# A post-norm decoder layer with routed experts: weights split by GpSimd beside the experts, a later order of units, and gate maxima spread by TensorE

## The reference

```
x = LN(x + Attn(x))                        # 16 batches x 128 tokens x 256, 16 heads of 64
x = LN(x + mLSTM(q=x, k=v=ctx))            # 4 heads of 64, gates from 3*256 features
   log_f = log_sigmoid(fg); cs = cumsum(log_f)
   log_d[t,s] = cs[t] - cs[s] + ig[s]  (s <= t);  m = max_s log_d;  d = exp(log_d - m)
   c = (q @ k.T / 8) * d;  h = c / (max(sum c, exp(-m)) + eps) @ v;  RMS norm per head
xn = LN(x) * gamma + beta;  probs = softmax(xn @ Wr + br);  top 2 of 8 experts
full[e] = relu(xn @ W1[e] + b1[e]) @ W2[e] + b2[e]      # W1 256x1024, W2 1024x256
c = relu(b1) @ W2 + b2;  out = sum_k score_k * (full[idx_k] - c[idx_k] + sum_e c_e)
x = LN(x + x + out)
```

## Time and profile before

| | us |
|---|---|
| runs | 919.39, 920.82, 922.27 (median 920.82) |
| profiled execution, its own time | 924.46 |
| its span, first to last instruction | 922.6 |
| PE / DVE / ACT / POOL busy | 710.0 / 441.9 / 331.3 / 307.8 |
| mean granted TensorE clock | 0.859 |

### The profile page before, as it was taken

The page is one execution under the profiler, slowest core; times in us unless marked ns, Lnnn a source line. Parts: engine busy times, 40 slices in busy tenths (PEclk is TensorE's granted clock), DMA queues, the critical chain, the costliest instruction groups (busy, mean ns, idle before and its releaser), DMA issues.

```text
span 922.6 us, 14727 instructions
## 1 busy us (share of the span) xinstructions
PE 710.0 (77%) x4774; PEld 600.5 (65%) x4775; DVE 441.9 (48%) x906; ACT 331.3 (36%) x994; POOL 307.8 (33%) x416
## 2 busy tenths in 40 slices
PE   5898898888787987986553102999999999699762
PEld 4788787778676785865443001788888888588421
DVE  3334444465363654647266600555555555255354
ACT  4565656656465565664121000222121212121100
POOL 3156335353645526356434174000000000000572
PEclk9899989989798999999555555999999999899755
DMA  9756454453434534354355432117427311510242
GB/s 308 281 184 191 130 160 149 138 162 108 131 104 153 165 98 129 94 164 138 105 226 205 195 107 80 35 58 286 183 83 295 149 40 40 227 35 24 69 142 75
DMA packets 87141, 130.22 MB, mean 141 GB/s; under 512 B 9856, under 2 KB 72752, under 8 KB 86064
## 3 DMA queue, kind: packets, MB, share of 16 engines
q1 hardware_dynamic: 81664, 83.36, 28.2%
q0 software_dynamic: 5408, 46.15, 13.1%
q10 hardware_dynamic: 16, 0.01, 0.0%
HBM read 79.12 MB, written 50.36 MB: 140 GB/s over the span
## 4 chain that ended last, share of the span: by engine, by line
PE 43%; POOL 14%; issue 14%; DMA 14%; DVE 9%; SPq 5%; ACT 1%; POOLq 0%; DVEq 0%; ACTq 0%
PE bank L881 11%; DMA w_dram<-w_pair 8%; PE bank L852 4%; PE bank L854 4%; PE bank L853 4%; PE bank L862 3%; POOL arena L654 3%; POOL w_pair L552 3%; PE bank L664 3%; PE bank L666 2%; PE bank L665 2%; POOL w_pair L550 2%; PE bank L805 2%; DMA y_dram<-work 2%; DMA w_raw<-in_L_ffn_b_dram 2%
## 5 line engine op out<-in xcount | busy, mean ns | idle before, releaser
L550 POOL CAST w_pair<-work 128x256 fp32r<-128x256 f32 x128 | 60.8, 475 | 184.1 <-DMA w_dram<-w_pair 164.5
L881 PE MATMUL bank<-w_ring,hidT_hi 128*128 x320 | 119.7, 408 | 1.3 <-DVE hidT_lo L1403 1.3
L1071 ACT ACTIVATE hidT_hi<-bank 128x512 fp32r<-128x512 f32 x80 | 43.6, 596 | 181.5 <-PE bank L862 181.5
L552 POOL TENSOR_TENSOR w_pair<-work,w_pair 128x256 fp32r<-128x256 f32 x128 | 103.0, 805 | 10.2
L994 ACT ACTIVATE arena<-bank,negmx 128x128 f32<-128x128 f32 x256 | 90.8, 375 | 20.8 <-DVE negmx L1108 20.8
L881 PE MATMUL bank<-w_ring,hidT_lo 128*128 x320 | 83.3, 281 | 0.0
L1376 DVE TENSOR_TENSOR arena<-bank,w_raw 128x512 f32<-128x512 f32 x80 | 55.3, 692 | 49.6 <-PE bank L854 48.8
L852 PE MATMUL bank<-w_ring,xgT_hi 128*128 x160 | 68.7, 430 | 11.3 <-DMA w_raw<-in_L_ffn_b_dram 8.5
L555 POOL DMA_DIRECT2D w_ring<-w_dram x8 | 4.7, 590 | 217.4 <-PE bank L881 217.4
L881 PEld LDWEIGHTS bank<-w_ring,hidT_hi 128*128 128x128 f32 x320 | 60.1, 188 | 12.9 <-issue 1.8
L1382 DVE TENSOR_REDUCE work<-bank 128x256 f32<-128x512 f32 x40 | 27.7, 692 | 80.9 <-PE bank L881 71.2
(11 more groups left out here) (215 smaller groups left out, 1854.2 us busy)
## 6 DMA issues: line engine op xcount, KB each, us to landing
w_dram<-w_pair SPq DMA_DIRECT2D x128, 256.0 KB, 2.3
w_ring<-w_dram POOLq DMA_DIRECT2D x8, 4096.0 KB, 12.9
work<-in_L_ffn_W_dram SPq DMA_DIRECT2D x128, 128.0 KB, 2.8
xg_dram<-work SPq DMA_DIRECT2D x10, 512.0 KB, 8.9
work<-xg_dram SPq DMA_DIRECT2D x40, 128.0 KB
y_dram<-work SPq DMA_DIRECT2D x40, 128.0 KB, 1.7
work<-gmax_dram SPq DMA_DIRECT2D x16, 256.0 KB, 3.9
w_raw<-in_L_ffn_b_dram POOLq DMA_DIRECT2D x8, 512.0 KB, 14.0
```

Of the source, the lines that this page charges most:

```text
L550: pool.tensor_copy(hi, raw).then_inc(w_rounded, 1)
L552: pool.tensor_tensor(lo, raw, hi.bitcast(F32), ALU.subtract).then_inc(w_split, 1)
L881: last = pe.matmul(o, l, r, start=c == 0 and l is both[0], stop=c == FC - 1 and l is both[0])
L1071: nc.scalar.activation(hidT_hi[:, par, 4 * half:4 * half + 4, :], bank[3 + half][:, :].rearrange("p (c t) -> p c t", c=4), ACT.Relu)\
```

## The change

The weights no longer pass through DRAM. `w_dram`, `gmax_dram`, the parts, `spread_maxima` and their buffers go. GpSimd loads an expert's raw weights into `w_raw` (two halves, W1 and W2, 1 MB each) and splits a half in one cast and one subtraction of 128x2048, straight into `w_ring`. The biases move to the place of `wq_lo`. The maxima are spread by a new unit B: four products of a 4x128 selector with gmax, into a ring bank which the decays then read. The lists of units, ScalarE's cut of them and VectorE's order change too.

```diff
             if s == 0:
-                return (of("S", i - 2) + of("k", i, 2) + of("q", i, 2) + of("w", i - 1, 1, 0),
-                        of("w", i - 1, 1, 1) + of("q", i, 3) + of("k", i, 3) + of("N", i - 4))
+                return (of("k", i, 2) + of("q", i, 2) + of("w", i - 1, 1, 0),
+                        of("w", i - 1, 1, 1) + of("q", i, 3) + of("S", i - 2) + of("k", i, 3) + of("N", i - 4))
             if s == 1:
-                return (of("v", i, 1, 0) + of("T", i - 2),
-                        of("v", i, 0, 1) + of("v", i, 1, 1) + of("L", i - 4) + of("X", i - 1) + of("C", i - 1))
+                return (of("v", i, 1, 0) + of("B", i - 2, 0),
+                        of("v", i, 0, 1) + of("B", i - 2, 1) + of("v", i, 1, 1) + of("L", i - 4) + of("T", i - 2))
             if s == 2:
-                return (of("x", i + 1, 0) + of("x", i + 1, 1) + of("G", i - 1) + of("q", i + 1, 0) + of("k", i + 1, 0),
-                        of("q", i + 1, 1) + of("k", i + 1, 1))
+                return (of("x", i + 1, 0) + of("x", i + 1, 1) + of("X", i - 1) + of("C", i - 1)
+                        + of("q", i + 1, 0) + of("k", i + 1, 0), of("q", i + 1, 1) + of("G", i - 1) + of("k", i + 1, 1))
...
# GpSimd
-            def load_expert(e):
-                pool.dma_start(w_ring[:, e % RING, :], w_dram[e]).then_inc(w_loaded, 16)
-                pool.dma_start(b1_rep[:, e % RING, :], b1[e:e + 1, :].broadcast_to([P, F])).then_inc(w_loaded, 16)
+            def load_raw(e, part):
...
+            def load_bias(e):
+                if e > 0:
+                    pool.wait_ge(b1_loaded, 16 * e)
+                pool.dma_start(b1_rep[:, e % RING, :], b1[e:e + 1, :].broadcast_to([P, F])).then_inc(b1_loaded, 16)
+
+            def split(e, part):
...
+                pool.wait_ge(w_loaded[part], 16 * e + 16)
+                pool.tensor_copy(both[:, :, 0, :], raw).then_inc(w_rounded, 1)
+                pool.wait_ge(w_rounded, 2 * e + part + 1)
+                pool.tensor_tensor(both[:, :, 1, :], raw, both[:, :, 0, :].bitcast(F32), ALU.subtract)\
+                    .then_inc(w_split, 1)
+                if e + 1 < E:
+                    pool.wait_ge(w_split, 2 * e + part + 1)
+                    load_raw(e + 1, part)
             def mask(p, b):
-                pool.wait_ge(decay_done, 2 * p + b + 1)
+                read(pool, ("B", p, b))
...
                     if s == 3 and 0 <= i - 3 < PAIRS:
                         scale_xn(i - 3)
+                    if (i, s) == (PAIRS - 1, 2):
+                        done(pool, ("v", PAIRS - 1, 1, 1))
+                        for part in range(2):
+                            load_raw(0, part)
+                    if (i, s) == (PAIRS - 1, 3):
+                        split(0, 0)
                     if (i, s) == (PAIRS, 1):
-                        load_expert(0)            # and experts 1 and 2 at (9, 1) and (10, 3)
+                        for k in range(RING):
+                            load_bias(k)
+                        split(0, 1)
+                    if (i, s) == (PAIRS, 2):
+                        split(1, 0)
                     if (i, s) == (PAIRS + 2, 3):
+                        split(1, 1)
+                        for part in range(2):
+                            split(2, part)
...
             for e in range(RING, E):              # each behind y_done of expert e - 3
-                load_expert(e)
+                load_bias(e)
+                for part in range(2):
+                    split(e, part)
# TensorE
+                elif kind == "B":
...
+                    for h in range(XH):
+                        last = pe.matmul(dst[:, h * S:(h + 1) * S], pick_head[:, h, :], gmax[:, b * S:(b + 1) * S],
+                                         start=True, stop=True)
             def hidden(j, par, half, e):
-                    pe.wait_ge(w_loaded, 32 * e + 32)
+                    pe.wait_ge(b1_loaded, 16 * e + 16)
+                    pe.wait_ge(w_split, 2 * e + 1)
             def expert_out(j, par, e, look):
+                pe.wait_ge(w_split, 2 * e + 2)
# ScalarE: decays(un) runs in the place of B's copy
-                    last = nc.scalar.activation(dec[:, b, h, :], dec[:, b, h, :], ACT.Exp,
+                    last = nc.scalar.activation(dec[:, b, h, :], ring(un)[0][:, h * S:(h + 1) * S], ACT.Exp,
...
-                    cut = {0: len(before) - 2, 1: 0, 2: 2, 3: 2}[s] if i < PAIRS else 0
+                    split = {0: 1, 1: 1, 2: 4, 3: 2}[s] if i < PAIRS else 0
+                    if s == 3 and 0 <= i - 1 < PAIRS:
+                        soft_gates(i - 1)         # was at the end of step 2
# VectorE, in step order
-                    if s == 1: weigh(i - 2)       # first in step 1
-                    if s == 2: read_gates(i - 1)  # ahead of add_heads
+                    if s == 3: both_norms(i - 3)  # now ahead of gate_sums(i - 1)
                     if n + 1 < STEPS * PAIRS:
                         weights_of(n + 1)
+                    if s == 1 and 0 <= i - 2 < PAIRS:
+                        weigh(i - 2)
+                    if s == 2 and 0 <= i - 1 < PAIRS:
+                        read_gates(i - 1)
```

More of the change, by code:

```diff
@@ L109, in decoder_layer @@
         w_raw = sb("w_raw", [P, W_WORDS])
+        wq_lo_at = nc.sbuf_base
         wq_lo = sb("wq_lo", [P, KC, INNER], F32R)
@@ L296, in decoder_layer @@
         gmax_ready = sem("gmax_ready")
-        gmax_stored = sem("gmax_stored")
+        pick_ready = sem("pick_ready")
         m_ready = sem("m_ready")
         em_ready = sem("em_ready")
-        mrep_loaded = [sem(f"mrep_loaded{k}") for k in range(2)]
-        decay_done = sem("decay_done")
         masked = sem("masked")
@@ L319, in decoder_layer @@
         scattered = sem("scattered")
-        part_loaded = [sem(f"part_loaded{k}") for k in range(4)]
-        pair_stored = [sem(f"pair_stored{k}") for k in range(2)]
-        w_loaded = sem("w_loaded")
+        w_loaded = [sem(f"w{k + 1}_loaded") for k in range(2)]
+        b1_loaded = sem("b1_loaded")
         w_rounded = sem("w_rounded")
@@ L432, in _ @@
                     .then_inc(zeros_stored, 16)
[L433 to L477, removed]
             for i in range(LAST):
@@ new lines, in load_bias @@
+            def load_bias(e):
[3 more added lines that the diff above has]
+            def split(e, part):
+                n = (512, D)[part]
+                half = slice(part * W_WORDS, (part + 1) * W_WORDS)
+                both = w_ring[:, e % RING, half].rearrange("p (g k n) -> p g k n", k=2, n=n)
+                raw = w_raw[:, part * KC * F:(part + 1) * KC * F].rearrange("p (g n) -> p g n", n=n)
+                pool.wait_ge(w_loaded[part], 16 * e + 16)
[6 more added lines that the diff above has]
+                    load_raw(e + 1, part)
@@ L599, in _ @@
                         rstd_of_pair(i - 1)
-                    if i < PAIRS:
-                        for k in range(PER_STEP * s, PER_STEP * (s + 1)):
-                            split_part(i, k)
                     if s == 2 and 0 <= i - 3 < PAIRS:
@@ L985, in copies @@
                 for un in part:
-                    if un[0] not in "wGT":
+                    if un[0] == "B":
+                        decays(un)
+                    elif un[0] not in "wGT":
                         copy_unit(un)
@@ L1035, in _ @@
                     before, after = fillers(i, s)
-                    cut = {0: len(before) - 2, 1: 0, 2: 2, 3: 2}[s] if i < PAIRS else 0
-                    if s == 1 and 0 <= i - 2 < PAIRS:
-                        decays(i - 2, 1)
-                    copies(before[:cut])
+                    split = {0: 1, 1: 1, 2: 4, 3: 2}[s] if i < PAIRS else 0
+                    if s == 3 and 0 <= i - 1 < PAIRS:
+                        soft_gates(i - 1)
+                    copies(before[:split])
                     if n + 1 < STEPS * PAIRS:
                         exponentials(n + 1, 0)
-                    copies(before[cut:])
+                    copies(before[split:])
                     if i < PAIRS:
@@ L1052, in _ @@
                                        ps_oT.rearrange("p (c t) -> p c t", c=4)).then_inc(oT_rounded, 1)
-                    if s == 0 and 0 <= i - 2 < PAIRS:
-                        decays(i - 2, 0)
-                    if s == 2 and 0 <= i - 1 < PAIRS:
-                        soft_gates(i - 1)
                     if s == 3 and 0 <= i - 1 < PAIRS:
@@ L1271, in _ @@
                         head_sums(i - 3)
-                    if s == 1 and 0 <= i - 2 < PAIRS:
-                        weigh(i - 2)
                     if s == 1 and 0 <= i - 1 < PAIRS:
```

70 lines of the change are left out of this document (27 added, 43 removed).

## The result

The changed kernel takes **940.04 us** (median of 5 runs, 939.24 to 946.69), the kernel before 920.82: ratio 1.0225, 95% interval 1.0197 to 1.0254. It is slower by 19.2 us, 14 us more than forecast. The profiled execution, from which all rows of after come, took 946.69 (span 944.9), 6.7 us above its median; that of before was 3.6 above its own.

The account below looks back on a forecast made before the run. TensorE bounds loop and experts, a chain of small operations the stretch between. 924.46 − 5 + 14 + 7 − 10 + 1 = 931.5, less 3.6 to the median and 2 shading: 926 us, range 896 to 945.

Parts of the forecast that it names:

- Part 1: Pair loop: weights leave it, ending four N waits (13.8 us) and lower clock behind them (9 us); gain 23 us.
- Part 2, waits: Pair loop, late iteration: new TensorE waits of 1.7 (v), 0.6 (T), 2.7 (X) and 2 us (k3).
- Part 2, clock: Pair loop: iteration 54.9 us beside 54.75, loop −5; −30 if waits stay hidden, +8 if each costs clock.
- Part 3a: Behind the loop: three splits ahead of the iotas delay the scatters by 14 us; ends +12 to +19.
- Part 3b: Chain to `weigh(7)` behind the loop: bias loads, splits and VectorE's norms behind them cost +7 us; ends −2 to +13.
- Part 4: Experts: wait for last expert's weights falls from 8.5 to 1.4 us, −10; register waits +1; ends −11 to +4.
- A: Loop really gets shorter, −30 us, as waits overlap and the clock stays up; 897 us, chance 0.35.
- C: Loop iterations reach 57 us through late rstd, and every tail split blocks VectorE; 952 us, chance 0.12.
- B: Gains and costs cancel: loop gains 8 us and VectorE gets the port behind it; 920 us, chance 0.15.
- The lock: SBUF port: GpSimd's splits exclude VectorE operations with two SBUF inputs or in 2-port mode, up to 4.5 us each.

Follow-up runs that it names:

- 887.9 us kernel: The kernel before with only the new weight path, three splits moved behind the 32 scatters and bias loads behind the iotas: 887.9 us, ratio 0.967.

## Why the prediction was right, and where it was wrong

The direction was right, and the time lies inside the wide range (896 to 945), 4 us past the forecast's own (919 to 936). Of the 15 us between the forecast's 931.5 us and the 946.7 of the profiled execution, the loop makes 9.9, the chain to `weigh(7)` 6.4, the splits 3.0, less 4 from the experts.

- **Part 1** (gain 23 us in the loop). N's waits went as said. Alone, the weight path gave 15.5 us in all, and with it six iterations took 303.4 instead of 328.5 us: 25 us, near the forecast's 23, but partly by luck: the forecast put all of it on the four iterations with N, which gained 18.5 us (224.7 to 206.2), and nothing on the first two, which gained 6.6. Some 10 us of it were lost again behind it: late splits and bias loads gave 17.4 more (887.9).
- **Part 2, waits.** Expected 1.7 (v) + 0.6 (T) + 2.7 (X) + 2 (k3) = 7.0 us per iteration; measured 1.3 + 0.4 + 1.2 + 2.2, and 1.3 for the transposes that I did not name: 6.4 us. A B unit was 1.15 us in a record, and its pair 2.0 us of TensorE's time against 1.8.
- **Part 2, clock: the step that failed.** I counted 48.4 + 1.8 − 2.3 = 47.9 us of busy time, as if N's waits alone cost clock and the new ones did not, and said in the same paragraph that the end "if each also costs clock" was +8. It was near that end: 51.4 us busy at the same clock of 0.91 as with N's wait, of which S ahead of q3 takes back 2.7, and 58.1 us from X to X, past the 53 to 57 named as the sign. The prediction also read the clock too short: 0.91 of 58 us is some 5 us lost, but about 10 us at the lower level, as the windows of 4 and 7 us show. The loop came to +4.9 in the profiled execution where −5 was forecast. In the runs with late splits, with late bias loads and with gate_sums first, whose units stand in the same order, `read_wo(7,0)` began at 435.8, 430.0 and 429.5 us, from 3.5 behind to 2.8 ahead of the kernel before; so the term was out by 2 to 10 us. The 2 us by which the sum was shaded, as part 2 "could more easily be overstated", went the wrong way.
- **Part 3a** (+14). Measured +17.0, and −15.3 when undone. The split itself was right (1.9 + 4.5 us). I left out its end: GpSimd waits 0.30 us for the subtraction and issues the next raw load in 0.7 to 1.0 us, 7.6 us a split.
- **Part 3b** (+7, ends −2 to +13). Measured +13.4, past the upper end. The chain of 41 us was right: normalise(7) to `weigh(7)` took 41.25 us (458.95 to 500.20). The wait of `gate_sums(7)` behind `both_norms(5)` was named in it, and cost 7.4 us when undone. What failed is the 9 us by which pair 7's normalise was to come earlier: counted from `read_wo(7,0)` it is 4.1 us (21.8 instead of 25.9). Not seen were the scans of pair 6 behind split(0,0), 6.57 instead of 0.73 us, behind which TensorE's next w unit waits 10.3 us. Nor was it seen that the order alone, with no split in the chain, makes the stretch 7.9 us shorter (in its one profiled execution), so that the splits and bias loads cost it 21 us.
- **Part 4** (−10). Measured −13. The first product with the last expert's weights waits 1.25 us; 1.4 was forecast. The two more waits per tile cost nothing that shows.
- **The rivals.** A (897) was the weight path with the old order, not this one: there the loop was 31 us shorter (`read_wo(7,0)` at 401.3), where A had 30. C's size in the loop (iterations of 57 us) was nearly met, but its cause wasn't: `rstd` behind the masks makes X wait only 1.2 us. B (920) is met by no run: the order alone takes 919.9 us, but it has none of B's splits, so the number is chance.

The lock, last. In the 887.9 us kernel the two instructions of VectorE's normalise, tensor_scalar with one large SBUF input, took 6.54 us beside a GpSimd cast and subtraction. In the changed kernel the experts' additions (L1348, one input from PSUM, one from SBUF) took 0.691 us on average, as long as before (0.692), and eight of them lie wholly inside a subtraction, at 0.69 us each. The Trainium skill (SBUF — State Buffer, Who interferes with whom) says both: a 2-port mode and two SBUF inputs are kept out for the whole instruction, one SBUF input outside such a mode is not. By that rule the traces agree, though no row says in which mode the tensor_scalar ran.

What stays open: why weight path and order cost 36 us together that neither costs alone. The three splits and the bias loads are hardly part of it, as the weight path alone pays for them too: 17.4 us, from 905.3 to 887.9, beside 15.3 and 4.0. In it are S between q3 and k3 (9.5), `gate_sums` behind `both_norms` (7.4), and the B units with the rest of the order (13.4 on the new weight path, where the whole order cost nothing on the old one). No run shows why these cost nothing while the parts went through DRAM. In the loop, the order with the parts in DRAM had iterations of 53.8 to 57.9 us at a clock of 0.90 to 0.97, and the order without them 58.1 at 0.91. The sum of the waits does not tell them apart: in one iteration each, TensorE is idle for 6.8 us, but busy for 48.4 us at 0.97 there and 51.4 us at 0.91 here. The waits lie elsewhere (7.6 us in four for k3 and 7.2 for the transposes, instead of 9.0 and 5.1). S ahead of q3 also brings the clock back to 0.97. So where the waits lie, or how long single ones are, matters; no run separates the two.

## What to carry to other kernels

Price a new wait of TensorE with the clock behind it: here 0.7 us less waiting per iteration gave 3.4 us back, 2.7 of them as busy time of the same instructions. Before moving big instructions of one engine out of a busy loop, ask what stands behind them in its queue where they land, and which engine they keep out: the three splits cost 15.3 us in front of the iotas and nothing that shows behind the scatters, where they run beside the first tiles (585 to 607 us) and no product waits for their weights. And a DMA that nobody waits for is not worth replacing by work on the engine that bounds the loop: the B units cost 12 us.

## What was not expected of the hardware

The same instructions take different times from one execution to the next, by the clock alone. The first iteration after X(0) is the same in the changed kernel (the first row of this text: 50.31 us, clock 0.93) and in the one with late bias loads:

```profile
89.15:137.21 48.06, 43.71 (x384) 37.88 (x385) 21.24 (x41) 29.71 (x101) 1.95 (x3) 1.00 0.02 6
```

A granted clock of 1.00 instead of 0.93 is worth 2.25 us of 50. Differences of 3 us between two kernels cannot be read from one profiled execution of each.
